# A five-layer decoder on one core: rotary halves moved by transfers, and constants of the recurrence moved into bias operands

## The reference

```python
def apply_rope(x, cos, sin):          # on the keys, 64 features of a head
    x1, x2 = (x[..., :d2], x[..., d2:])
    return jnp.concatenate([x1 * cos - x2 * sin, x2 * cos + x1 * sin], axis=-1)
...
attn = jnp.einsum('bhnd,bhsd->bhns', q, k) * scale
attn = jax.nn.softmax(jnp.clip(attn, -11.0, 11.0), axis=-1)
...
u = x @ Wi.T + bi                     # recurrence: 256 steps, 8 sequences side by side
sp = x @ Ws.T + bs
def step(state, inp):
    state = jnp.tanh(state @ A.T + u_t @ B.T) + sp_t
    return (state, state @ C.T)
out = ys @ Wo.T + bo
...
out = att @ dense_w + dense_b         # linear attention, then layer norm
```

## Time and profile before

| what | value |
|---|---|
| three runs | 1147.28, 1149.36, 1156.16 us |
| the profiled execution | 1147.91 us, its span 1146.1 us, mean granted clock 0.889 |
| PE busy in the span | 966.1 us (84%) |
| DVE, ACT, POOL busy | 682.3 (60%), 500.3 (44%), 494.0 us (43%) |
| chain that ended last | PE 61%, DVE 20%, ACT 6%, POOL 5%, issue 3%, SPq 3%, DMA 2% |

### The profile page before, as it was taken

The page is one execution under the profiler, slowest core; times in us unless marked ns, Lnnn a source line. Parts: engine busy times, 40 slices in busy tenths (PEclk is TensorE's granted clock), DMA queues, the critical chain, the costliest instruction groups (busy, mean ns, idle before and its releaser), DMA issues.

```text
span 1146.1 us, 21485 instructions
## 1 busy us (share of the span) xinstructions
PE 966.1 (84%) x8233; PEld 665.1 (58%) x8233; DVE 682.3 (60%) x1923; ACT 500.3 (44%) x1412; POOL 494.0 (43%) x615
## 2 busy tenths in 40 slices
PE   3658999998999999899899999988844899999811
PEld 2435666666665666666666575655533677677501
DVE  3356676657657766875776777575555123433478
ACT  3636654563564565466456455633310222332200
POOL 1035366356446545644644654566531012222351
PEclk8689999999899999999999999999975877877755
DMA  6000000000000000000000000000000011111400
GB/s 175 20 1 6 11 1 5 11 1 5 2 10 1 5 11 1 6 11 1 1 5 11 2 1 1 2 1 20 1 1 0 4 16 18 20 23 18 54 7 37
DMA packets 60396, 15.06 MB, mean 13 GB/s; under 512 B 41334, under 2 KB 59526, under 8 KB 60166
## 3 DMA queue, kind: packets, MB, share of 16 engines
q1 hardware_dynamic: 60294, 13.69, 6.0%
HBM read 10.51 MB, written 3.17 MB: 12 GB/s over the span
## 4 chain that ended last, share of the span: by engine, by line
PE 61%; DVE 20%; ACT 6%; POOL 5%; issue 3%; SPq 3%; DMA 2%; POOLq 0%; DVEq 0%
PE score_banks L1650 8%; PE out_bank L1622 7%; PE bank_a L1410 5%; PE score_banks L1429 5%; PE score_banks L1810 5%; DVE o_rec L1130 5%; DVE prob L1158 3%; PE score_banks L1454 3%; PE bank_d L1505 3%; PE score_banks L1431 3%; PE out_bank L1605 3%; PE score_banks L1430 3%; PE bank_d L1823 3%; PE out_bank L1630 2%; PE score_banks L1749 2%
## 5 line engine op out<-in xcount | busy, mean ns | idle before, releaser
L851 ACT ACTIVATE prob<-score_banks 128x1024 f32<-128x1024 f32 x128 | 131.0, 1023 | 166.0 <-PE score_banks L1650 165.8
L1650 PE MATMUL score_banks<-qh,kr 64*128 64x256 f32 x1024 | 149.6, 412 | 3.1 <-ACT qh L819 2.7
L664 POOL TENSOR_TENSOR psum<-psum,prob 128x512 f32<-128x512 f32 x64 | 81.6, 1276 | 156.7 <-DVE prob L1158 156.7
L1130 DVE RECIPROCAL o_rec<-out_bank 128x256 f32<-128x256 f32 x64 | 111.9, 1748 | 30.6 <-PE out_bank L1630 30.6
L662 POOL TENSOR_TENSOR psum<-prob 128x512 f32<-128x512 f32 x64 | 83.0, 1297 | 102.6 <-DVE prob L1158 102.6
L1622 PE MATMUL out_bank<-prob,v 128*64 128x256 f32 x1024 | 124.7, 386 | 1.3 <-DVE on L1131 1.3
L1650 PEld LDWEIGHTS score_banks<-qh,kr 64*128 64x128 f32 x1024 | 91.2, 191 | 41.8 <-issue 32.4
L791 ACT ACTIVATE prob<-prob,neg_max 128x128 f32<-128x128 f32 (+1 forms) x256 | 107.1, 426 | 12.9 <-DVE neg_max L1030 12.9
L1158 DVE TENSOR_SCALAR prob<-prob 128x1024 f32<-128x1024 f32 x128 | 101.2, 791 | 18.4 <-ACT prob L851 18.4
L902 ACT ACTIVATE prob<-score_banks 128x8 f32<-128x8 f32 x255 | 45.2, 177 | 121.5 <-PE score_banks L1810 121.5
L1622 PEld LDWEIGHTS out_bank<-prob,v 128*64 128x64 f32 x1024 | 67.8, 136 | 46.6 <-issue 17.2
(11 more groups left out here) (340 smaller groups left out, 2114.3 us busy)
## 6 DMA issues: line engine op xcount, KB each, us to landing
cb<-in_ctx_dram SPq DMA_DIRECT2D x8, 256.0 KB, 2.8
bias_mask<-bias_scratch SPq DMA_DIRECT2D x1, 1536.0 KB, 7.4
xb<-in_x_dram SPq DMA_DIRECT2D x8, 128.0 KB, 2.1
prob<-in_L_xattn_Wkv_dram SPq DMA_DIRECT2D x1, 1024.0 KB, 7.1
x_scratch<-v SPq DMA_DIRECT2D x16, 64.0 KB, 1.5
att_scratch<-on SPq DMA_DIRECT2D x16, 64.0 KB, 1.5
prob<-att_scratch SPq DMA_DIRECT2D x16, 64.0 KB, 2.9
out_dram<-v SPq DMA_DIRECT2D x4, 256.0 KB, 2.5
```

What stands on the lines that cost most here:

```text
L664: link(g.tensor_tensor(psum[:, p % 2, :], psum[:, p % 2, :], pp[:, 2, :], ALU.add))
L851: s.activation(prob[:, p % 2, 2 * u:2 * u + 2, :].rearrange("p k (h q) -> p h k q", h=2), sc[:, 0:2, :].rearrange("p h (k q) -> p h k q", ...
L1130: link(w.reciprocal(o_rec[:, :], bank[:, T:2 * T]))
L1650: last = mm(sc[:, h, k * T:(k + 1) * T], kr[rows_of, p % 2, kb * P:(kb + 1) * P], qh[rows_of, p % 2, :], start=True, stop=True, skip_group ...
```

## The change

1. **Keys.** "keys a" and "keys b" become one job "keys" with `wk_s` only; `wkx_s` and what made it go. DVE makes `k_cos` as before, then clamp(0), and directly behind it `k_raw` = bank x signed sines, not yet exchanged; only then is the bank given back. SP copies `k_raw` into `k_sin` by four transfers inside SBUF, 32 rows x 512 (64 KB) each, with the halves of each head exchanged. POOL's `rotate` waits for the four transfers. The loads of `xb` and `cb` are woven between these transfers, and the matrices come behind the last of them. The signs of the sines are flipped to suit.
2. **Constants of the recurrence.** `c_rows` and `one_row` go. The two constants stand in `z_bias`, one value per partition, and every tanh has one of its columns as bias operand. `z_of` has two products in place of four; the z work of steps 64 to 255 takes halves in 24 steps in place of thirds in 36.
3. **Bias rows.** The bias products of `inputs_of` (i = 0) and `dense` (i = 6) take 128-row operands (a first column of the unit matrix spread over 64 columns, and a bias laid out on all rows) in place of one-row ones.
4. **Fillers.** For t >= 64 a filler of 96 columns is added behind the side work of every step except i = 0 and 6; the shorter filler in steps without side work ends at t = 24 in place of 36.

```diff
     if p == PAIRS - 1:
-        return {} if last else {"keys a": 1, "values 0": 0, "values 1": 0, "queries": 0, "keys b": 1}
+        return {} if last else {"keys": 1, "values 0": 0, "values 1": 0, "queries": 0}
     if p + 2 < PAIRS or not last:
-        target["keys a"] = (p + 2) % PAIRS
+        target["keys"] = (p + 2) % PAIRS
     target["queries"] = p + 1
-    if p + 2 < PAIRS or not last:
-        target["keys b"] = (p + 2) % PAIRS
...
+SWAPS = 4 * 16
...
-        wkx_s = sb("wkx_s", [P, 2, INNER], F32R)
...
+        k_raw = sb("k_raw", [P, S])
...
-        bias_row = x_t[0:1, 0:D]
-        one_row = sin_t[0:1, :]
-        c_rows = rec_t[0:1, 0:2 * D]
+        pre_bias = x_t[:, 0:D]
+        first_row = rec_t[:, 0:HALF_ROWS]
...
             0, 4, 5, 6, 7, 8, 9, 10, 11, 13, 15)
...
+            def swap_halves(key):
+
+                sp.wait_ge(p_free["dve"], KEYS_DONE[key])
+                if key >= 1:
+                    sp.wait_ge(kr_ready, key)
+                for lo in range(0, P, HALF):
+                    other = lo + HALF if lo % DH == 0 else lo - HALF
+                    sp.dma_start(k_sin[lo:lo + HALF, :], k_raw[other:other + HALF, :]).then_inc(k_swapped, 16)
+
+            load_x(0, 1)
+            load_ctx(0, 1)
+            swap_halves(0)
+            swap_halves(1)
+            for b in range(B):
+                for p in range(PAIRS):
+                    if p == 1 and b + 2 < B:
+                        load_x(b + 1, b + 2)
+                    if p == 4 and b + 2 < B:
+                        load_ctx(b + 1, b + 2)
+                    if p + 2 < PAIRS or b + 1 < B:
+                        swap_halves(n(b, PAIRS, p) + 2)
...
             def rotate(key):
 
-                pool.wait_ge(p_free["dve"], KEYS_DONE[key])
+                pool.wait_ge(k_swapped, SWAPS * (key + 1))
                 g.tensor_tensor(kr[:, key % 2, :], k_cos[:, :], k_sin[:, :], ALU.add).then_inc(kr_ready, 1)
...
-            g.memset(one_row, 1.0).then_inc(ident16_ready, 1)
...
-                swapped = "c (h t d) -> c t h d"
                 s.activation(wk_s[:, 0, :], wkv_nat[:, 0:INNER], ACT.Identity)
-                for t in range(2):
-                    s.activation(wkx_s[:, 0, :].rearrange(swapped, t=2, d=HALF)[:, t],
-                                 wkv_nat[:, 0:INNER].rearrange(swapped, t=2, d=HALF)[:, 1 - t], ACT.Identity)
...
             act.wait_ge(c_ready, 1)
-            s.activation(hid[:, 0:B], cf[:, 0:B], ACT.Tanh).then_inc(h_ready, 1)
+            act.wait_ge(td_free, 3)
+            s.activation(hid[:, 0:B], cf[:, 0:B], ACT.Tanh, bias=z_bias[:, 0:1]).then_inc(h_ready, 1)
             def step(t):
                 act.wait_ge(z_ready, t)
-                s.activation(hid[:, t * B:(t + 1) * B], cf[:, t * B:(t + 1) * B], ACT.Tanh).then_inc(h_ready, 1)
+                s.activation(hid[:, t * B:(t + 1) * B], cf[:, t * B:(t + 1) * B], ACT.Tanh,
+                             bias=z_bias[:, 1:2]).then_inc(h_ready, 1)
...
-                dve.wait_ge(p_full, job.full)
                 bank = prep_bank[job.bank][:, :]
-                if part == "a":
+                if part == "cos":
+                    dve.wait_ge(p_full, job.full)
                     if key >= 1:
                         dve.wait_ge(kr_ready, key)
-                    w.tensor_tensor(k_cos[:, :], bank, cos_t[:, :], ALU.mult).then_inc(p_free["dve"], 1)
+                    w.tensor_tensor(k_cos[:, :], bank, cos_t[:, :], ALU.mult)
                 else:
-                    w.tensor_tensor(k_sin[:, :], bank, sin_t[:, :], ALU.mult).then_inc(p_free["dve"], 1)
+                    if key >= 1:
+                        dve.wait_ge(k_swapped, SWAPS * key)
+                    w.tensor_tensor(k_raw[:, :], bank, sin_t[:, :], ALU.mult).then_inc(p_free["dve"], 1)
...
                 w.tensor_tensor(wk_s[:, 1, :], wkv_nat[:, 0:INNER], wk_s[:, 0, :].bitcast(F32), ALU.subtract)
-                for t in range(2):
-                    view = [wkx_s[:, k, :].rearrange(swapped, t=2, d=HALF)[:, t] for k in range(2)]
-                    w.tensor_tensor(view[1], wkv_nat[:, 0:INNER].rearrange(swapped, t=2, d=HALF)[:, 1 - t],
-                                    view[0].bitcast(F32), ALU.subtract)
...
+                    keys_job("cos")
                     clamp(0)
+                    keys_job("sin")
                     slots(0, 1)
                     slots(1, 2)
...
                     clamp(1)
                     slots(2, 3)
-                    keys_job("b")
                     slots(3, 4)
                     slots(4, 5)
...
+            w.tensor_copy(z_bias[:, 0:1], bank_d[:, 3 * D:3 * D + 1])
+            w.tensor_copy(first_row, ident[:, 0:1].broadcast_to([P, HALF_ROWS])).then_inc(td_free, 1)
             dve.wait_ge(td_full, 3)
             w.tensor_tensor(gws_t, bank_d[:, 0:D], ident[:, :], ALU.add)
-            w.tensor_copy(c_rows[:, D:2 * D], bank_d[0:1, D:2 * D])
-            w.tensor_copy(bias_row, bank_d[0:1, 2 * D:3 * D]).then_inc(td_free, 1)
+            w.tensor_copy(z_bias[:, 1:2], bank_d[:, D:D + 1])
...
-                weights = wk_s if part == "a" else wkx_s
-                split_mm(bank[:, :], weights[:, 0, c], weights[:, 1, c], cn_s[:, b % 2, 0, :],
+                split_mm(bank[:, :], wk_s[:, 0, c], wk_s[:, 1, c], cn_s[:, b % 2, 0, :],
...
-                        prep("keys b", prep_keys, "b")
...
-            mm(bank_d[0:1, D:2 * D], cols[:, BI_COL:BI_COL + 1], b_t, start=True, stop=False, skip_group_check=True)
-            mm(bank_d[0:1, D:2 * D], cols[:, BS_COL:BS_COL + 1], a_t, start=False, stop=True, skip_group_check=True)
-            mm(bank_d[0:1, 2 * D:3 * D], cols[:, BS_COL:BS_COL + 1], g_t, start=True, stop=False, skip_group_check=True)
-            mm(bank_d[0:1, 2 * D:3 * D], cols[:, BO_COL:BO_COL + 1], ident[:, :], start=False, stop=True,
-               skip_group_check=True).then_inc(td_full, 1)
+            mm(bank_d[:, D:D + 1], b_t, cols[:, BI_COL:BI_COL + 1], start=True, stop=False, skip_group_check=True)
+            mm(bank_d[:, D:D + 1], a_t, cols[:, BS_COL:BS_COL + 1], start=False, stop=True, skip_group_check=True)
+            to_all = [P, P]
+            mm(bank_d[:, 2 * D:3 * D], cols[:, BS_COL:BS_COL + 1].broadcast_to(to_all), g_t, start=True, stop=False,
+               skip_group_check=True)
+            mm(bank_d[:, 2 * D:3 * D], cols[:, BO_COL:BO_COL + 1].broadcast_to(to_all), ident[:, :], start=False,
+               stop=True, skip_group_check=True).then_inc(td_full, 1)
...
 
                 bank = cf[:, lo:hi]
                 mm(bank, bwi_t, x3_t[:, lo:hi], start=start, stop=False, skip_group_check=True)
                 skip = B if lo == 0 else 0
-                mm(bank[:, skip:], aws_t, x3_t[:, lo + skip - B:hi - B], start=False, stop=False,
-                   skip_group_check=True)
-                last = mm(bank[:, skip:], c_rows[:, D:2 * D], one_row[:, skip:hi - lo], start=False, stop=True,
+                return mm(bank[:, skip:], aws_t, x3_t[:, lo + skip - B:hi - B], start=False, stop=True,
                           skip_group_check=True)
-                if skip:
-                    last = mm(bank[:, 0:B], c_rows[:, 0:D], one_row[:, 0:B], start=False, stop=True,
-                              skip_group_check=True)
-                return last
...
+            def bias_of_rows(bank, row, **kw):
+                for of in halves:
+                    last = mm(bank[of, 0:D], first_row, row, skip_group_check=True, **kw)
+                return last
...
-                product_of_rows(bank_d, one_row[:, 0:P], bias_row, start=False, stop=False)
+                bias_of_rows(bank_d, pre_bias, start=False, stop=False)
...
-                product_of_rows(bank_d2, one_row[:, 0:P], b_dense[0:1, :], start=False,
-                                stop=True).then_inc(dense_full, 1)
+                bias_of_rows(bank_d2, b_dense[:, :], start=False, stop=True).then_inc(dense_full, 1)
...
                 worked = window(k, i)
-                if t <= 3 * Z_PARTS:
-                    z_third(*divmod(t - 1, 3))
+                if t <= 2 * Z_PARTS:
+                    z_half(*divmod(t - 1, 2))
                 if not worked:
-                    keep_clock(KEEP_Z if t <= 3 * Z_PARTS else KEEP, bank_d2 if t < Z_FIRST // B else sc[:, 0, :])
+                    keep_clock(KEEP_Z if t <= 2 * Z_PARTS else KEEP, bank_d2 if t < Z_FIRST // B else sc[:, 0, :])
+                elif t >= Z_FIRST // B and i not in (0, 6):
```

51 lines of the change are left out of this document (23 added, 28 removed).

## The result

The changed kernel took 1157.09 us (median of 20 runs, 1152.78 to 1161.2), the kernel before 1152.12 (20 runs, 1140.25 to 1156.57). The ratio is 1.0051, with a 95% interval of 1.0031 to 1.0071: slower by half a per cent, inside what the text calls no change. The forecast was 1156.0, range 1133 to 1174, with "same" as the likeliest.

A forecast was written before the change was run, and what follows sets the result against it. It took a batch to change between PE as the limit and DVE with POOL. Terms 2.4 + 0.8 + 2.7 + 1.7 + 0.3 = +7.9 on the profiled 1147.9 us gave 1155.8; it said 1156.0, range 1133 to 1174.

The forecast's parts named there:

- What bounds the kernel: Main stage: a batch changes between places where PE is the limit and places where DVE and POOL are.
- Keys, +0.4 us a batch and +0.8 in the last: Main stage: removed matmuls against the moved sine product; +0.4 us a batch, +2.4 in all, +0.8 in the last batch.
- of which I take two as on the path, 1.2 us: Main stage: of the sine products at pairs 6, 7 and 0, 0.6 us each, two lengthen a batch, 1.2 us.
- 6 full transitions: Main stage, batch to batch: the net +0.4 us is counted 6 times, +2.4 us.
- The transfers: Key exchange, taken as 3.8 us: hidden in the loop at no cost; not hidden in the set-up, net +2.7 us there.
- The clock of the main stage, +1.7: Main stage: PE's waits grow, and one further fall of its clock costs +1.7 us, bounds 0 and +10.
- The operand, +0.09 us a step: Recurrence: the tanh's bias operand takes a plain step from 0.565 to 0.655 us, in 223 steps.
- Fillers and full rows, +0.3 with z_of: Recurrence: fillers hold the clock in most windows, 175.2 us, +1.4; with z_of's -1.1 the stage comes to +0.3.
- PE as the bound (1129): Main stage: PE bounds it after all and half of the 51 us is realised, -20.9 us, about 1129; chance 0.12.
- The free operand (1135): Recurrence: the tanh's operand costs nothing and the clock is held, -14.1 us in all, about 1135; chance 0.14.
- The unheld clock (1170): Recurrence: the operand costs 0.09 us and the clock stays where it was, +21 us in all, about 1170; chance 0.24.
- Late transfers: Loop and set-up: slow issues make the key transfers late, +20 and +10 us, about 1187; chance 0.04.

The follow-up runs named there:

- e6_pe_cut: The kernel before with two of the three matmuls of every keys b job left out; 1147.59 us against 1148.88, ratio 1.0000.
- e12_cut_hold: e9_hold with two of the three matmuls of every keys b job left out; 1103.82 us, ratio 0.9655 to the kernel before.
- e1_keys: The kernel before with part 1 of the change (keys) alone; 1165.94 us against 1148.92, ratio 1.0149.
- e3_products: e2_rec with the recurrence's constants brought in by 128-row products and no bias operand on the tanh; 1121.83 us, ratio 0.9757 to the kernel before.
- e2_rec: The kernel before with parts 2 to 4 of the change (recurrence) alone; 1142.09 us, ratio 0.9943.
- e8_one_row: e2_rec with the bias products of i = 0 and 6 on one row again; 1151.11 us, ratio 1.0033 to the kernel before.
- e4_no_fill: e2_rec without the fillers behind the side work (t >= 64); 1158.64 us, ratio 1.0091 to the kernel before.
- e5_sin_late: e1_keys with the product with the sines put back behind the second clamp; 1256.81 us, ratio 1.0922 to the kernel before.
- e10_after_products: The changed kernel with the recurrence's constants by full-row products in place of the tanh's bias operand; 1138.16 us, ratio 0.9914 to the kernel before.
- e9_hold: e3_products with fillers of 192 columns in two of PE's waits in the main stage; 1109.72 us, ratio 0.9684 to the kernel before.

## Why the prediction was right

The number was within 1.1 us of the median, and that is in part luck. Between the two profiled executions the forecast had +7.9 us and +10.1 came (1146.1 to 1156.2 of span); between the medians it is +5.0. By terms, forecast and measured: set-up +2.7 and +4.4; seven batches +2.4 for the keys and +1.7 for the clock, together +4.1, and +11.6; last batch +0.8 and -0.8; up to tanh 0 -1.1 and -1.8; the recurrence +1.4 and -3.6; the rest 0 and +0.3. So the batches were 7.5 us too cheap and the recurrence 5 too dear, and the two errors cancelled for the most part.

- **What bounds the kernel.** Right: a batch is a chain that changes engines. e6_pe_cut and e12_cut_hold show it. The 94% of PE would have said 29 us for the two matmuls; they gave 0 and 3 to 6 in the total.
- **Keys, +0.4 us a batch and +0.8 in the last.** Right in kind, too small by far: +2.4 was forecast for the batches, and with the clock held it is about 12. With the clock held the keys cost 1.5 us a batch (96.7 against 95.2), with it free 97.8 against 96.3 in the mean of the seven of e1_keys and of before, again 1.5. What failed is "of which I take two as on the path, 1.2 us": beside the 1.3 us of the sixth interval (10.7 to 12.0) there are 0.5 in the first, 0.3 in the third, 0.1 in the fifth and 0.6 in the seventh, against 0.6 in the fourth and 0.7 in the last. "6 full transitions" failed too: the seventh costs 2.9. The last batch gained 0.8 in place of losing it, and 1.7 where both have their clock at 1.00. One sign of the prediction did not come: the wait at L1505 grew from 2.1 to 2.6 us and not to 3.6.
- **The transfers.** Right in the loop: no wait of POOL there, landing in 2.0 us between the 1.5 and 2.9 of the earlier trace rows. In the set-up the second kr began at 94.44, where the forecast's sequence puts it at 95.1. The net of +2.7 was measured as +4.4. What failed is "the clamp(1) and the ctx statistics behind it absorb about 2.1": from the first k_cos to the first reciprocal it is 26.7 us in place of 21.5, so of the 5.9 only 0.7 were absorbed. The first k_cos came 0.8 earlier, near the 1.0 forecast for the weights.
- **The clock of the main stage, +1.7.** The falls of the clock are there, as the holding fillers show, but they are no new cost of the change: filling the waits shortened the seven batches by 13.1 us with the keys of before and by 13.3 with those of the change. This term should have been about 0.
- **The operand, +0.09 us a step.** Right: 0.268 against 0.177. The forecast paid it in 223 steps, 20 us; e3_products against e2_rec shows it in all 255, with 23.9 us less recurrence, because the steps i = 0 and 6 are not bound by PE either. That the two kernels differ by 20.3 is near this 20 by chance. Here the Trainium skill's rule on pointer operands (ScalarE: Activation LUTs, "What ACT_TABLE_LOAD costs", about 93 ns each) and this case's 91 ns agree, and e3_products shows the loop paying it in full.
- **Fillers and full rows, +0.3 with z_of.** It came to -5.4, so it was off by 5.7 us to the good side. The step that failed is "the after has 32 steps of 0.85 us (i = 0 and 6, bound by PE)": they take 0.655, as every other. The 0.85 was read from one-row products and carried over to those on 128 rows; e8_one_row shows that it comes with the one row. That alone is 32 x 0.195 = 6.2 us. The clock was held entirely from step 64 on (1.00), and stayed low only for steps 32 to 63, where no filler stands behind side work (windows of 11.8 and 11.9 us). The 173.8 us of the old recurrence, from which the term is counted, were the lowest of five profiles of it, so against the medians the gain is larger: e2_rec shows 6.8 us.
- **The rivals.** PE as the bound (1129): refuted. The free operand (1135): refuted. The unheld clock (1170): it is what e4_no_fill shows, at 1158.6 with the keys of before, but the fillers prevent it. Late transfers: they did not come in the loop, and e5_sin_late shows that they would with the sines one step later.

So the change holds a gain of 27 us, fillers and full rows, as e3_products shows it. It gives some 20 of these to the tanh's operand and 15 to 17 to the keys (15.0 between e2_rec and the changed kernel, 16.3 between e3_products and e10_after_products, 17.0 in e1_keys), and ends slower. e9_hold keeps the gain alone and holds the clock in the main stage as well: 3.2% under the kernel before, and 3.7% by the ratios under the changed one.

What stays open: that it is the place of the sines that makes a batch 1.5 us longer is read from the chain and the intervals, and no run moves them without another change (e5_sin_late made the transfers late); why the clock falls in one batch and not in the next at the same instruction; and what fillers would give in the last batch or behind the side work of steps 32 to 63.

## What to carry to other kernels

In a loop of two engines with a period of half a microsecond, count every operand: a constant that saves a few matmuls outside the loop but adds a bias column to its instruction cost 0.09 us at every turn here. Work taken off the busiest engine pays only between the waits of the chain (here 0.9 of 3.7 us a batch), and the clock may take even that back elsewhere, when PE stands idle for longer. Fillers that nothing reads, put into such a wait, are a small edit, and gave 8 to 12 us here. When work is moved from the busiest engine to a transfer, look at what the transfer forces early on the engines that feed it.

## What was not expected of the hardware

- A product on one row between products on 128 rows costs some 0.2 us more than one on 128 rows, at the same number of columns and the same clock: starts 0.35 and 0.37 us apart around it, against 0.25 and 0.27. At 504 columns it is again 0.2, and the first weight load on one row begins 0.42 us later than one on 128 rows does, with its product and not ahead of it.
- Batches of the same code take one of a few values (95.2, 96.7, 98.2, 99.5 us), by whether the clock falls behind two waits of 2.1 and 2.4 us and for how long; with these waits filled the clock is 1.00, and every batch takes 95.2 us.
- With less work for it, PE can come to be busy for longer: in the last batch of e12_cut_hold 50.3 us in place of 48.5, at a clock of 0.89 in place of 0.97.
- Transfers inside SBUF of 64 KB on 32 rows landed 2.0 us behind the start of their issue in the median (1.9 to 3.8), of which 0.59 us are the issue.
